# Factorization-machine scorer on Trainium2: the weights, the parameters and the first columns of the input in one transfer instead of three

## The chip, the cores and the metric

The kernel runs on one core of one Trainium2 chip. The metric is the device time of one execution in microseconds (us); lower is better. On that core five engines run their own instruction streams and meet at semaphores: TensorE (PE, with its weight loads as PEld), VectorE (DVE), ScalarE (ACT), GpSimd (POOL) and SyncE (SP), which here issues every DMA transfer. Sixteen DMA engines carry the bytes.

## The reference

The input x is float32, 1024 samples by 12500 features. With a factor matrix F (12500 x 16), linear weights w (12500) and a small three-layer network (16 to 128 to 64 to 1):

```python
x_reg = x @ W_lin.T + b_lin
emb = x @ factors
sum_squared = jnp.square(emb.sum(axis=1))
squared_sum = (jnp.square(x) @ jnp.square(factors)).sum(axis=1)
h = relu(emb @ W1.T + b1)
h = relu(h @ W2.T + b2)
y = x_reg + 0.5 * (sum_squared - squared_sum)[:, None] + h @ W3.T + b3
return (0.5 + sigmoid(y) * 5.0).squeeze()
```

So each feature is multiplied by 17 weights (16 factors and the linear one), and its square by one weight, the row sum of the squared factors. x is 51.2 MB and is read once; everything else is small.

## The kernel before

x lies transposed in HBM, features on the 128 partitions. The 12500 features are 97 chunks of 128 and a remainder of 84. The first chunk (`xf`, 128 x 1024) and the remainder (`xl`, three sets of 32 features, laid out as 128 x 768) are handled ahead of everything. The other 96 chunks come in groups of 8 chunks by 512 samples, 2 MB each: 12 groups for the first half of the samples, then 8 for the second half. They go through a ring `xr` of RING = 4 slots. The last 32 chunks of the second half come as nine smaller end pieces (`x_end`, PIECES) of 352 or 160 samples.

For a group, TensorE multiplies the 8 chunks by their 17 weights into the bank `p_lin` of that half (L467), while VectorE squares three chunks (L394) and ScalarE five (L298) into `sq`; TensorE then multiplies the squares into the same bank. GpSimd copies each group's weights into `wr` (L273) and the row sums of the squared factors into `wz` (L275). After the squares' last matmul TensorE increments `sq_used`, and SP, which waits for it, refills the slot (L242). The half's network layers and the sigmoid follow, for the second half in two blocks of samples, and the result is stored.

SP's queue before the loop holds, in this order: the head `hd` (L232: the weights of all 97 chunks, the parameters of the network, the weights of the remainder; 128 rows of 7616 B), `xf` (L233: 128 rows of 4096 B), `xl` (L234: 128 rows of 3072 B) and the four first groups (L236: 128 rows of 16384 B each). Each has its own semaphore: `hd_landed`, `first_landed`, `rest_landed`, `x_landed[s]`.

What waits for the three first transfers: VectorE waits for `hd_landed`, computes the squared factors `fsq` (L376), those of the remainder, their row sums `s_all` (L381) and `ws`, the bias (L385), waits for `rest_landed` and squares the remainder (`sql`, L388); then come its groups. ScalarE waits for `first_landed` and squares the first chunk (`sqf`, L290). GpSimd waits for `hd_landed` and for the row sums, copies them to `ws` (L266, L267), and then places weights for the ring. TensorE clears its banks, waits for `hd_landed` and `first_landed` and multiplies the first chunk; waits for `rest_landed` and multiplies the remainder; then the squares of both; then the groups.

Of the kernel before, what the change touches and what calls it, by code (L numbers as in the profile page):

```python
# [6 lines left out]
ACT = mybir.ActivationFunctionType  # L7
# [5 lines left out]
B, N, EMB = 1024, 12500, 16  # L13
H1, H2 = 128, 64
P = 128
LIN = EMB + 1
# [22 lines left out]
REST_K = 32  # L39
REST_SETS = -(-REST // REST_K)  # L40
REST_COLS = B // (P // REST_K)
# [32 lines left out]
C_ALL = C_HALF + 4  # L74


HD_P = ALL * LIN
HD_L = HD_P + C_ALL
HD = HD_L + REST_SETS * LIN


def fm_kernel(nc, head, x_first, x_rest, x_groups, x_end, out):
    with ExitStack() as ctx:
        def sb(name, shape, dt=F32):
            return ctx.enter_context(nc.sbuf_tensor(name, shape, dt))
# [4 lines left out]
        def sem(name):  # L90
            return ctx.enter_context(nc.semaphore(name))

        hd = sb("hd", [P, HD])
        xf = sb("xf", [P, B])
        xl = sb("xl", [P, REST_SETS, REST_COLS])
        xr = sb("xr", [P, RING, CHUNKS, HALF])
        sqf = sb("sqf", [P, B])
        sql = sb("sql", [P, REST_SETS, REST_COLS])
# [11 lines left out]
        rest = sb("rest", [P, BLOCKS[2][1]])  # L110
# [7 lines left out]

        w = hd[:, 0:HD_P].rearrange("p (c k) -> p c k", k=LIN)
        pr = hd[:, HD_P:HD_L]  # L120
        wl = hd[:, HD_L:HD].rearrange("p (c k) -> p c k", k=LIN)

        p_lin = [bank("p_lin0"), bank("p_lin1")]
        p_sq = bank("p_sq")
# [2 lines left out]
        p_h2 = bank("p_h2")  # L127

        hd_landed = sem("hd_landed")
        first_landed = sem("first_landed")  # L130
        rest_landed = sem("rest_landed")
        x_landed = [sem(f"x_landed{s}") for s in range(RING)]
        end_landed = [sem(f"end_landed{i}") for i in range(len(PIECES))]
        y_stored = sem("y_stored")
# [8 lines left out]
        first_squared = sem("first_squared")  # L143
# [28 lines left out]
        def cols(k):  # L172

            c, n = BLOCKS[k]
            return slice(c, c + n)
# [21 lines left out]
        def tot_bank(k):  # L197
            return p_tot[k % 2]
# [5 lines left out]
        def width(i):  # L204
            return BLOCKS[PIECES[i][0]][1]

        def piece(a, i, c, n):

            at = ENDS * (BLOCKS[PIECES[i][0]][0] - HALF)
            return a[:, at + c * width(i):at + (c + n) * width(i)]  # L210
# [5 lines left out]
        def chunks(i):  # L216
            return sum(PIECES[i][2]) + sum(PIECES[i][3])

        def last_slot(i):
            k, c = PIECES[i][:2]  # L220
            return (ENDS * (BLOCKS[k][0] - HALF) + (c + chunks(i)) * BLOCKS[k][1] - 1) // (CHUNKS * HALF)
# [8 lines left out]
        @block.sync  # L230
        def _(sp):
            sp.dma_start(hd[:, :], head).then_inc(hd_landed, 16)  # L232
            sp.dma_start(xf[:, :], x_first).then_inc(first_landed, 16)  # L233
            sp.dma_start(xl[:, :, :].rearrange("p c b -> p (c b)"), x_rest).then_inc(rest_landed, 16)  # L234
            for s in range(RING):
                sp.dma_start(xr[:, s].rearrange("p c b -> p (c b)"), x_groups[s, :, 0:CHUNKS * HALF]).then_inc(x_landed[s], 16)  # L236

            with sp.Fori(1, sum(ROUNDS)) as r:
                for s in range(RING):

                    sp.wait_ge(sq_used, RING * r + s + 1)
                    sp.dma_start(xr[:, s].rearrange("p c b -> p (c b)"),  # L242
                                 x_groups[bass.ds(RING * r + s, 1), :, 0:CHUNKS * HALF].rearrange("g p n -> (g p) n")
                                 ).then_inc(x_landed[s], 16)
            at = 0
            for i in range(len(PIECES)):
                c, n = PIECES[i][1], chunks(i)
                rows = x_end[at:at + P * n * width(i)].rearrange("(p m) -> p m", p=P)
                sp.wait_ge(sq_used, TOTAL + last_slot(i) + 1)
                sp.dma_start(piece(xe, i, c, n), rows).then_inc(end_landed[i], 16)  # L250
                at += P * n * width(i)

            for k in range(len(BLOCKS)):
                sp.wait_ge(y_ready[k], 1)
                sp.dma_start(out[cols(k)].rearrange("(q b) -> q b", q=4), y[0:P:32, line(k)]).then_inc(y_stored, 16)
            sp.wait_ge(y_stored, 16 * len(BLOCKS))
# [28 lines left out]
        @block.scalar  # L285
        def _(act):
            act.wait_ge(zero_set, 1)
            nc.scalar.activation(warm[:, :], zero[:, 0:1], ACT.Sigmoid)
            act.wait_ge(first_landed, 16)
            nc.scalar.activation(sqf[:, :], xf[:, :], ACT.Square).then_inc(first_squared, 1)  # L290

            def squares(r, s):
                act.wait_ge(x_landed[s], 16 * (r + 1))

                act.wait_ge(sq_used, RING * r + s + 1)
                c = BY_DVE
                for n in BY_ACT:
                    nc.scalar.activation(sq[:, s, c:c + n, :], xr[:, s, c:c + n, :],  # L298
                                         ACT.Square).then_inc(act_squared, 1)
                    c += n  # L300

            def square_end(i, j=0):
                c = PIECES[i][1] + sum(PIECES[i][2][:j])
                n = PIECES[i][2][j]
                if j == 0:
                    act.wait_ge(end_landed[i], 16)
                nc.scalar.activation(piece(sq_end, i, c, n), piece(xe, i, c, n),  # L307
                                     ACT.Square).then_inc(act_end_squared, 1)

            def copy_lin(k, u):  # L310
                nc.scalar.copy(lin[:, part(k, u)], p_lin[k][:, u * BLOCKS[k][1] // 2:(u + 1) * BLOCKS[k][1] // 2]  # L311
                               ).then_inc(lin_ready[k], 1)

            def layer1(k, n):
                act.wait_ge(p_h1_done[k], 1)
                c = BLOCKS[k][0]
                nc.scalar.activation(h1[:, c:c + n], p_h1[0][:, 0:n], ACT.Relu,
                                     bias=pr[:, C_B1:C_B1 + 1]).then_inc(h1a_ready[k], 1)

            def embedding_square(k):  # L320
                act.wait_ge(p_es_done[k], 1)
                nc.scalar.activation(gsq[:, line(k)], tot_bank(k)[:, line(k)], ACT.Square).then_inc(gsq_ready[k], 1)

            def sigmoid(k):
                act.wait_ge(p_tot_done[k], 1)
                nc.scalar.activation(sg[:, line(k)], tot_bank(k)[:, line(k)], ACT.Sigmoid,
                                     bias=bias[:, :]).then_inc(sg_ready[k], 1)

            with act.Fori(0, ROUNDS[0]) as r:
                for s in range(RING):  # L330
                    squares(r, s)

            act.wait_ge(sq_used, RING + GROUPS)
            copy_lin(0, 0)
            copy_lin(0, 1)
            layer1(0, BLOCKS[0][1] // 2)
            embedding_square(0)
            act.wait_ge(bias_ready, 1)
            sigmoid(0)

            with act.Fori(ROUNDS[0], sum(ROUNDS)) as r:
                for s in range(RING):
                    squares(r, s)

            square_end(0, 0)
            square_end(0, 1)
            square_end(1, 0)
            square_end(1, 1)
            square_end(2)
            square_end(3)  # L350
            square_end(4, 0)
            act.wait_ge(p_lin_done[1], 1)
            copy_lin(1, 0)
            copy_lin(1, 1)
            nc.scalar.copy(rest[:, :], p_lin[1][:, BLOCKS[1][1]:HALF]).then_inc(rest_copied, 1)
            embedding_square(1)
            square_end(4, 1)
            layer1(1, BLOCKS[1][1])
            square_end(5, 0)
            square_end(5, 1)  # L360
            square_end(6, 0)
            square_end(6, 1)
            square_end(7, 0)
            square_end(7, 1)
            square_end(8)
            sigmoid(1)
            embedding_square(2)
            act.wait_ge(squares_done, 1)
            nc.scalar.copy(qs[:, :], p_sq[:, 0:BLOCKS[LAST][1]]).then_inc(qs_ready, 1)
            sigmoid(2)  # L370

        @block.vector
        def _(dve):
# [10 lines left out]
                                    ).then_inc(s_ready, 1)  # L384
            nc.vector.tensor_tensor(bias[:, :], pr[:, C_BLIN:C_BLIN + 1], pr[:, C_B3:C_B3 + 1],  # L385
                                    ALU.add).then_inc(bias_ready, 1)
            dve.wait_ge(rest_landed, 16)
            nc.vector.tensor_tensor(sql[:, :, :], xl[:, :, :], xl[:, :, :], ALU.mult).then_inc(rest_squared, 1)  # L388

            def squares(r, s):  # L390
# [74 lines left out]
        def _(pe):  # L465
# [15 lines left out]
                return ps[32 * (t % 4):32 * (t % 4) + m, c:c + n]  # L481

            pe.wait_ge(hd_landed, 16)
            pe.wait_ge(first_landed, 16)
            for h in range(2):
                add_mm(quad(p_lin[h], 0, LIN, 0, HALF), w[:, 0, :], xf[:, half(h)])

# [5 lines left out]
                        h, at = divmod(REST_COLS * t, HALF)  # L493
                        add_mm(quad(p_lin[h], t, m, at, REST_COLS), weights[rows, c, :], rhs[rows, c, :])

            pe.wait_ge(rest_landed, 16)
            remainder(LIN, wl, xl)
            pe.wait_ge(ws_ready, 1)
            pe.wait_ge(first_squared, 1)
# [220 lines left out]
```

## Time and profile before

| what | value |
|---|---|
| median of three runs | 134.57 us (134.57 to 134.70) |
| profiled execution | 134.6 us, span 132.4 us from first to last instruction |
| instructions | 2859 |
| TensorE busy | 106.6 us (81%), 1123 matmuls |
| ScalarE, VectorE, GpSimd busy | 64.1, 53.1, 12.5 us |
| DMA | 52.34 MB in 4639 packets, mean 395 GB/s over the span |
| DMA issues | head 952 KB, first chunk 512 KB, remainder 384 KB, 20 groups of 2048 KB, nine end pieces |

How to read it: the span is what the profile covers of one execution; the 2.2 us between it and the time lie around it. Busy time is an average over the span; where a chain of waits goes through DMA, an engine's idle time before it costs nothing. A timeline row gives the start, the duration, the engine, the line of the code, what is written from what, the number of instructions merged into the row, and in brackets how long the engine was idle before it and what ended that.

### The profile page before, as it was taken

To read this page: it belongs to the slowest core of one execution; us is meant where nothing else is said; L and a number is where in the kernel's file an instruction comes from. 1 tells how busy PE (TensorE), PEld (TensorE's weight loads), DVE (VectorE), ACT (ScalarE), POOL (GpSimd) and SP (SyncE) were. 2 spreads that over 40 slices of the span, in tenths; PEclk is the share of its full clock that TensorE was granted. 3 is DMA by queue.
4 is the path that set the end of the run, shared out by engine and by line. 5 is a ranking of instruction groups with operands and counts; after the bars stand their busy time and mean duration, and the time that the engine had idled before them with its cause. 6 is when DMAs were issued, how large, how long until landed. Compare 5 with 4: busy or idle time off the path is not lost.

```text
span 132.4 us, 2859 instructions
## 1 busy us (share of the span) xinstructions
PE 106.6 (81%) x1123; PEld 31.6 (24%) x1123; DVE 53.1 (40%) x51; ACT 64.1 (48%) x72; POOL 12.5 (9%) x48
## 2 busy tenths in 40 slices
PE   6089999768877877877978869996967966989992
PEld 4012222111111211211212312211111111335881
DVE  0392450532531541540540292450451351576571
ACT  4031660734733743742744394652662562465851
POOL 4016001110010011011011001151000000000000
PEclk9999999999999999999999999999999999999998
DMA  4999999999999999999999999999999999999800
GB/s 115 397 460 431 430 431 426 430 426 431 421 435 426 435 426 416 440 426 431 431 426 426 426 430 426 421 440 416 435 421 431 435 418 424 411 411 411 321 13 6
DMA packets 4639, 52.34 MB, mean 395 GB/s; under 512 B 532, under 2 KB 664, under 8 KB 1688
## 3 DMA queue, kind: packets, MB, share of 16 engines
q1 hardware_dynamic: 4632, 52.23, 93.6%
q8 instruction: 6, 0.10, 0.3%
q14 instruction: 1, 0.01, 0.0%
HBM read 52.22 MB, written 0.00 MB: 394 GB/s over the span
## 4 chain that ended last, share of the span: by engine, by line
DMA 63%; PE 28%; SPq 3%; ACT 3%; issue 2%; DVE 1%; ACTq 0%
DMA xr<-in_x_groups 52%; PE p_lin L467 22%; DMA xr<-in_x_end 11%; ACT sq L298 2%; PE p_sq L467 2%; PE p_h L557 2%; SPq L236 1%; PE p_tot L467 1%; PE p_h L588 1%; DVE h L419 0%; DVE h L414 0%; PE p_tot L570 0%; SPq L234 0%; SPq L233 0%; SPq L232 0%
## 5 line engine op out<-in xcount | busy, mean ns | idle before, releaser
L298 ACT ACTIVATE sq<-xr 128x1536 f32<-128x1536 f32 (+1 forms) x40 | 48.5, 1262 | 47.2 <-DMA xr<-in_x_groups 47.2
L394 DVE TENSOR_TENSOR sq<-xr 128x1536 f32<-128x1536 f32 x20 | 35.1, 1758 | 56.6 <-DMA xr<-in_x_groups 56.6
L467 PE MATMUL p_lin<-xr,wr 128*17 128x512 f32 x320 | 38.2, 594 | 13.8 <-DMA xr<-in_x_groups 13.8
L467 PE MATMUL p_lin<-sq,wz 128*18 128x512 f32 x320 | 38.2, 594 | 2.3 <-ACT sq L298 1.0
L467 PEld LDWEIGHTS p_lin<-xr,wr 128*17 128x17 f32 x320 | 7.9, 97 | 42.3 <-issue 21.6
L467 PEld LDWEIGHTS p_lin<-sq,wz 128*18 128x18 f32 x320 | 8.2, 97 | 31.5 <-ACT sq L298 16.9
L273 POOL COPY wr<-hd x20 | 7.4, 372 | 71.5 <-PE p_lin L467 70.8
L402 DVE TENSOR_TENSOR sq<-xr 128x320 f32<-128x320 f32 (+5 forms) x15 | 10.4, 724 | 8.1 <-DMA xr<-in_x_end 8.1
L307 ACT ACTIVATE sq<-xr 128x320 f32<-128x320 f32 (+5 forms) x15 | 9.1, 652 | 7.1 <-DMA xr<-in_x_end 7.1
L467 PE MATMUL p_lin<-xr,hd 128*17 128x352 f32 (+1 forms) x128 | 10.0, 380 | 1.5 <-DMA xr<-in_x_end 1.5
L467 PE MATMUL p_lin<-sq,ws 128*18 128x352 f32 x64 | 6.6, 459 | 0.0
L467 PE MATMUL p_lin<-xf,hd 128*17 128x512 f32 x4 | 3.6, 1049 | 3.5 <-DMA xf<-in_x_first 3.5
L467 PEld LDWEIGHTS p_lin<-xr,hd 128*17 128x17 f32 x128 | 4.3, 97 | 5.5 <-issue 3.6
L467 PE MATMUL p_sq<-sq,ws 128*18 128x160 f32 x64 | 4.1, 300 | 0.0
L275 POOL COPY wz<-s_all x20 | 3.9, 196 | 0.0
L376 DVE SCALAR_TENSOR_TENSOR fsq<-hd 128x1552 f32<-128x1552 f32 x1 | 1.8, 1775 | 4.4 <-DMA hd<-in_head 4.4
L290 ACT ACTIVATE sqf<-xf 128x1024 f32<-128x1024 f32 x1 | 1.1, 1057 | 4.7 <-DMA xf<-in_x_first 4.7
L467 PEld LDWEIGHTS p_lin<-sq,ws 128*18 128x18 f32 x64 | 2.4, 97 | 2.3 <-issue 1.4
L557 PE MATMUL p_h<-lin,hd 128*32 128x256 f32 (+2 forms) x32 | 2.4, 384 | 0.5 <-ACT lin L311 0.5
L467 PEld LDWEIGHTS p_sq<-sq,ws 128*18 128x18 f32 x64 | 2.5, 98 | 0.3
L414 DVE TENSOR_SCALAR h<-p_h,hd 128x256 f32<-128x256 f32 (+1 forms) x2 | 0.9, 434 | 4.0 <-PE p_h L557 4.0
L467 PE MATMUL p_lin<-xl,hd 32*17 32x256 f32 x24 | 2.3, 535 | 0.0
(50 smaller groups left out, 34.7 us busy)
## 6 DMA issues: line engine op xcount, KB each, us to landing
xr<-in_x_groups SPq DMA_DIRECT2D x20, 2048.0 KB, 15.4
xr<-in_x_end SPq DMA_DIRECT2D x1, 2112.0 KB, 10.8
xr<-in_x_end SPq DMA_DIRECT2D x3, 640.0 KB, 12.3
xr<-in_x_end SPq DMA_DIRECT2D x1, 1760.0 KB, 14.6
xr<-in_x_end SPq DMA_DIRECT2D x1, 1056.0 KB, 12.7
hd<-in_head SPq DMA_DIRECT2D x1, 952.0 KB, 4.8
xr<-in_x_end SPq DMA_DIRECT2D x1, 704.0 KB, 14.1
xf<-in_x_first SPq DMA_DIRECT2D x1, 512.0 KB, 5.7
```

What stands on the lines that cost most here:

```text
L236: sp.dma_start(xr[:, s].rearrange("p c b -> p (c b)"), x_groups[s, :, 0:CHUNKS * HALF]).then_inc(x_landed[s], 16)
L273: nc.gpsimd.tensor_copy(wr[:, bass.ds(s, 1), :, :].rearrange("p s c k -> p (s c) k"), w[:, bass.ds(at, CHUNKS), :]).then_inc(wr_ready, 1)
L275: nc.gpsimd.tensor_copy(wz[:, bass.ds(s, 1), :, LIN:WZ].rearrange("p s c k -> p (s c k)"), s_all[:, bass.ds(at, CHUNKS)]).then_inc(wz_read ...
L290: nc.scalar.activation(sqf[:, :], xf[:, :], ACT.Square).then_inc(first_squared, 1)
L298: nc.scalar.activation(sq[:, s, c:c + n, :], xr[:, s, c:c + n, :], ACT.Square).then_inc(act_squared, 1)
L307: nc.scalar.activation(piece(sq_end, i, c, n), piece(xe, i, c, n), ACT.Square).then_inc(act_end_squared, 1)
L376: nc.vector.scalar_tensor_tensor(fsq[:, :, :], w[:, :, 0:EMB], -0.5, w[:, :, 0:EMB], ALU.mult, ALU.mult).then_inc(fsq_ready, 1)
L394: nc.vector.tensor_tensor(sq[:, s, 0:BY_DVE, :], xr[:, s, 0:BY_DVE, :], xr[:, s, 0:BY_DVE, :], ALU.mult).then_inc(dve_squared, 1)
L402: nc.vector.tensor_tensor(piece(sq_end, i, c, n), piece(xe, i, c, n), piece(xe, i, c, n), ALU.mult).then_inc(dve_end_squared, 1)
L467: return nc.tensor.matmul(out, lhsT, rhs, start=False, stop=False, skip_group_check=True)
L557: mm = nc.tensor.matmul(bank[32 * t:32 * t + 32, 0:n], pr[:, C_W1 + 32 * t:C_W1 + 32 * t + 32], rhs, start=True, stop=True, skip_group_che ...
L588: mm = nc.tensor.matmul(p_h2[32 * t:32 * t + 32, row(k)], pr[:, C_W2 + t % 2 * 32:C_W2 + t % 2 * 32 + 32], h1[:, part(k, t // 2)], start=T ...
```

## The change

The first chunk and the remainder of x are put behind the weights in each of the head's 128 rows, which become 14784 B long. `xf` and `xl` are slices of the tile `hd`; the two transfers and their semaphores go, and each engine that waited for one of them has `hd_landed` instead, or nothing where it had that wait already. No other instruction changes.

```diff
 HD_P = ALL * LIN
 HD_L = HD_P + C_ALL
-HD = HD_L + REST_SETS * LIN
+HD_F = HD_L + REST_SETS * LIN
+HD_R = HD_F + B
+HD = HD_R + REST_SETS * REST_COLS
...
-        xf = sb("xf", [P, B])
-        xl = sb("xl", [P, REST_SETS, REST_COLS])
...
-        wl = hd[:, HD_L:HD].rearrange("p (c k) -> p c k", k=LIN)
+        wl = hd[:, HD_L:HD_F].rearrange("p (c k) -> p c k", k=LIN)
+        xf = hd[:, HD_F:HD_R]
+        xl = hd[:, HD_R:HD].rearrange("p (c b) -> p c b", b=REST_COLS)
...
             sp.dma_start(hd[:, :], head).then_inc(hd_landed, 16)
-            sp.dma_start(xf[:, :], x_first).then_inc(first_landed, 16)
-            sp.dma_start(xl[:, :, :].rearrange("p c b -> p (c b)"), x_rest).then_inc(rest_landed, 16)
...
-            act.wait_ge(first_landed, 16)
-            nc.scalar.activation(sqf[:, :], xf[:, :], ACT.Square).then_inc(first_squared, 1)
+            act.wait_ge(hd_landed, 16)
+            nc.scalar.activation(sqf[:, :], xf, ACT.Square).then_inc(first_squared, 1)
...
-            dve.wait_ge(rest_landed, 16)
             nc.vector.tensor_tensor(sql[:, :, :], xl[:, :, :], xl[:, :, :], ALU.mult).then_inc(rest_squared, 1)
...
             pe.wait_ge(hd_landed, 16)
-            pe.wait_ge(first_landed, 16)
...
-            pe.wait_ge(rest_landed, 16)
             remainder(LIN, wl, xl)
...
+    head[:, HD_F:HD_R] = xT[:P]
+    head[:, HD_R:] = rest.reshape(REST_SETS, REST_K, P // REST_K, REST_COLS).transpose(2, 1, 0, 3).reshape(P, -1)
```

## Rows read from the trace of the kernel before

**Rows 1.** The page: span, and gigabytes per second in 40 equal slices.
```profile
span 132.4 us, 2859 instructions
...
GB/s 115 397 460 431 430 431 426 430 426 431 421 435 426 435 426 416 440 426 431 431 426 426 426 430 426 421 440 416 435 421 431 435 418 424 411 411 411 321 13 6
```

**Rows 2.** The chain of waits in order of time: start us, us, what.
```profile
101.64 14.59 DMA xr<-in_x_end
...
116.28 6.75 PE p_lin L467 x92
```

**Rows 3.** VectorE's timeline: groups 1 to 4 and 20, then two end pieces.
```profile
12.87 1.76 DVE L394 TENSOR_TENSOR sq<-xr 128x1536 f32<-128x1536 f32 x1 [2.54 <-DMA xr<-in_x_groups]
17.78 1.76 DVE L394 TENSOR_TENSOR sq<-xr 128x1536 f32<-128x1536 f32 x1 [3.15 <-DMA xr<-in_x_groups]
23.86 1.76 DVE L394 TENSOR_TENSOR sq<-xr 128x1536 f32<-128x1536 f32 x1 [4.31 <-DMA xr<-in_x_groups]
28.76 1.76 DVE L394 TENSOR_TENSOR sq<-xr 128x1536 f32<-128x1536 f32 x1 [3.14 <-DMA xr<-in_x_groups]
...
107.08 1.76 DVE L394 TENSOR_TENSOR sq<-xr 128x1536 f32<-128x1536 f32 x1 [3.16 <-DMA xr<-in_x_groups]
...
122.15 0.90 DVE L402 TENSOR_TENSOR sq<-xr 128x320 f32<-128x320 f32 x2 [0.64 <-DMA xr<-in_x_end]
123.73 0.89 DVE L402 TENSOR_TENSOR sq<-xr 128x320 f32<-128x320 f32 x2 [0.69 <-DMA xr<-in_x_end]
```

**Rows 4.** The timeline of SP's issues.
```profile
0.75 0.40 SPq L232 DMA_DIRECT2D hd<-in_head  x1
...
1.66 0.44 SPq L234 DMA_DIRECT2D xl<-in_x_rest  x1
2.15 2.25 SPq L236 DMA_DIRECT2D xr<-in_x_groups  x4
19.83 3.76 SPq L242 DMA_DIRECT2D xr<-in_x_groups  x2
```

**Rows 5.** DMA queues: packets, MB, share of 16 engines over the span.
```profile
q8 instruction: 6, 0.10, 0.3%
```

**Rows 6.** DMA issues: size, median us from issue to landing.
```profile
xl<-in_x_rest SPq DMA_DIRECT2D x1, 384.0 KB, 6.2
```

**Rows 7.** The timeline of all engines from 0 to 26 us.
```profile
5.59 1.77 DVE L376 SCALAR_TENSOR_TENSOR fsq<-hd 128x1552 f32<-128x1552 f32 x1 [4.44 <-DMA hd<-in_head]
6.92 1.06 ACT L290 ACTIVATE sqf<-xf 128x1024 f32<-128x1024 f32 x1 [4.67 <-DMA xf<-in_x_first]
...
7.03 3.57 PE L467 MATMUL p_lin<-xf,hd 128*17 128x512 f32 x4 [3.51 <-DMA xf<-in_x_first]
...
9.38 0.95 DVE L388 TENSOR_TENSOR sql<-xl 128x768 f32<-128x768 f32 x1
9.46 0.91 POOL L266 COPY ws<-s_all 128x1 f32<-128x1 f32 x1 [7.57 <-DVE ws L383]
...
12.76 1.89 PE L467 MATMUL p_lin<-sqf,ws 128*18 128x512 f32 x4
...
15.99 1.91 PE L467 MATMUL p_lin<-xr,wr 128*17 128x512 f32 x16
...
23.86 1.91 PE L467 MATMUL p_lin<-xr,wr 128*17 128x512 f32 x16 [0.81 <-DMA xr<-in_x_groups]
```

**Rows 8.** Stretches: us, busy times, granted clock, DMA share, GB/s.
```profile
1.50:2.00 0.50, 0.50 (x4) 0.35 (x3) 0.00 (x0) 0.50 (x1) 0.40 (x1) 1.00 1.02 137
2.00:2.50 0.50, 0.50 (x5) 0.35 (x3) 0.00 (x0) 0.23 (x2) 0.00 (x0) 1.00 0.32 76
2.50:3.00 0.50, 0.50 (x4) 0.38 (x3) 0.00 (x0) 0.00 (x0) 0.00 (x0) 1.00 0.75 259
3.00:3.50 0.50, 0.50 (x3) 0.04 (x1) 0.00 (x0) 0.00 (x0) 0.00 (x0) 1.00 0.90 381
3.50:4.00 0.50, 0.02 (x1) 0.00 (x0) 0.00 (x0) 0.00 (x0) 0.00 (x0) 1.00 1.10 457
```

More of the change, by code:

```diff
@@ L78, with fm_kernel @@
 HD_L = HD_P + C_ALL
-HD = HD_L + REST_SETS * LIN
-def fm_kernel(nc, head, x_first, x_rest, x_groups, x_end, out):
+HD_F = HD_L + REST_SETS * LIN
+HD_R = HD_F + B
+HD = HD_R + REST_SETS * REST_COLS
+def fm_kernel(nc, head, x_groups, x_end, out):
     with ExitStack() as ctx:
@@ L129, in fm_kernel @@
         hd_landed = sem("hd_landed")
-        first_landed = sem("first_landed")
-        rest_landed = sem("rest_landed")
         x_landed = [sem(f"x_landed{s}") for s in range(RING)]
@@ L679 @@
     xT = np.asarray(r_input_data).T
-    x_first = np.ascontiguousarray(xT[:P])
     rest = np.zeros((REST_SETS * REST_K, B), f32)
     rest[:REST] = xT[P:P + REST]
-    x_rest = np.ascontiguousarray(rest.reshape(REST_SETS, REST_K, P // REST_K, REST_COLS).transpose(2, 1, 0, 3).reshape(P, -1))
     chunks = xT[P + REST:].reshape(ALL - 1, P, B)
@@ L711 @@
     params[:, C_B3] = np.asarray(L0_rec_b3)
-    arrays = {"head": head, "x_first": x_first, "x_rest": x_rest, "x_groups": x_groups, "x_end": x_end}
+    arrays = {"head": head, "x_groups": x_groups, "x_end": x_end}
     nc = bacc.Bacc("TRN2", target_bir_lowering=False, num_devices=1)
```

## The prediction

> **What bounds the kernel now.** I read the page first, for the shape of the span: of the 40 slices of the GB/s row, slices 2 to 37 read 397 to 460 [rows 1], so the 16 DMA engines have work from the second slice to the last 10 us. The question is whether a compute engine ever holds that stream up. The chain of waits answers it: its last DMA piece starts at 101.64 us, when SP issues the second end piece, and ends 14.59 us later, at 116.23 us, when that piece lands; from 116.28 us TensorE has it [rows 2]. A transfer of 1.8 MB that takes 14.59 us from issue to landing was queued behind others: VectorE's squares, which each wait for one group, start 4.89 or 4.90 us apart (28.76 minus 23.86; the 16 intervals from 28.76 to 107.08 us are 78.32 us, 4.895 us each, the copy work of the middle included) [rows 3]. So 2,097,152 B in 4.895 us, 428.4 GB/s, is the pace, and about three transfers stand in the queue at a time. SP's refill for slot 0 goes out at 19.83 us, while the groups that land at 23.86 and 28.76 us are still to come [rows 3, 4]: 8.9 us of cover.
>
> The end is therefore: start of the stream + all its bytes at 428.4 GB/s + a fixed tail of about 16 us behind the piece that lands at 116.23 us. The change keeps every byte: 7616 + 4096 + 3072 = 14784 B per row. Only three things can move the end: the start of the stream, the overhead of packets in it, or a compute engine that becomes so late that SP's refills are.
>
> One irregular row matters below. The third group comes 6.08 us after the second (23.86 minus 17.78), not 4.90, and no later interval gives the 1.18 us back [rows 3]. Compute was waiting, so this is in the stream. The queue rows give a candidate: six instruction fetches, 0.3% of 16 engines' 132.4 us, some 6.4 us in all or 1.06 us each [rows 5]. A group counts as landed when the last engine is through, so a fetch on one engine shows in every landing after it. That it was a fetch is my inference.
>
> **The change part by part.**
>
> *Two issues fewer on SP.* Before, SP issues the head at 0.75 us and the first group at 2.15 us [rows 4]. Without the two issues between, the first group goes out when the second transfer did, 0.75 + 0.40 + 0.05 = 1.20 us (0.05 is the gap between 1.66 + 0.44 and 2.15), 0.95 us earlier. That buys nothing while the queue is full: the three first transfers are 1,892,352 B, 4.42 us of streaming, so the first group's descriptors wait either way. If the stream did hang on the issue, it would be worth up to 0.95 us; I take 0.
>
> *256 data packets and 32 completion packets fewer.* From below 0. From the rows: head, first chunk and remainder land at 5.59 us (VectorE's first instruction on it), 6.92 us (ScalarE's square of the first chunk) and 1.66 + 6.2 = 7.86 us (issue and time to landing) [rows 4, 6, 7]. The first chunk took 1.33 us for 524,288 B, which at 428.4 GB/s would be 1.22; the remainder 0.94 us for 393,216 B, at that pace 0.92. Excess 0.11 + 0.02 = 0.13 us. The second estimate: two neighbouring end pieces of 640 KB (655,360 B, 5120 B rows) start VectorE at 122.15 and 123.73 us [rows 3], 1.58 us against 1.53 us at the pace, 0.05 us per transfer, 0.10 for two. I take 0.13 us off, bounds 0 and 0.2.
>
> The Trainium skill, *DMA: Bandwidth & Descriptors*, section on the anatomy of one DMA, fits a software-issued DMA with 2.0 us fixed plus its bytes; the same page advises to merge small transfers. Paid in series, that would take 4 us off and give 130.6 us. The trace disagrees for queued transfers: the second landed 1.33 us after the first, of which its bytes fill 1.22.
>
> *The start of the stream.* In the four half microseconds from 1.5 to 3.5 us it moves at 137, 76, 259 and 381 GB/s [rows 8]: 426 KB, where the pace would give 857 KB, so 431 KB or 1.0 us is lost in the ramp. The order of issue, rows and partitions of this first transfer stay; only its rows are 14784 B instead of 7616 B. If a stall is per row, fewer rows meet it and up to half, 0.5 us, comes back; if it is a latency in time, nothing does. Of the other sign, a longer row could hold a slow engine longer, by the 0.27 us that 7168 B more take on one engine at a sixteenth of the pace. I take 0: the ramp lasts as long as several rows, which looks like a time and not a count of rows (one of 7616 B takes an engine 0.28 us at a sixteenth of the pace, the ramp 1.5 us).
>
> *The head lands later.* All three waits become the one for 7.86 - 0.13 = 7.73 us. What stands behind it:
> - VectorE: from 5.59 us to the end of the remainder's square, 9.38 + 0.95 = 10.33 us, is 4.74 us [rows 7]. From 7.73 us it ends at 12.47 us. The first group lands at 12.87 - 0.13 = 12.74 us [rows 3]. Hidden with 0.27 us to spare; without that cover each us would delay the squares of the first group, not the stream.
> - GpSimd: its first copy of the row sums starts at 9.46 us, after the reductions [rows 7]; later by 7.73 - 5.59 = 2.14 us is 11.60 us, done at 12.51 us. TensorE wants it for the squares of the first chunk, at about 12.76 + 0.83 = 13.59 us [rows 7]. GpSimd's copies for the first slot follow and are wanted at about 16.8 us.
> - ScalarE: 1.06 us from 7.73 us, done at 8.79 us; nothing is due before 12.74 us.
> - TensorE: starts at 7.03 us now and at about 7.86 us then, 0.83 us later; its first group starts at 15.99 us now and at 16.8 us then. The first two groups go back to back, and then TensorE stands idle 0.81 us before the third group's matmuls at 23.86 us [rows 7], which wait for that landing, as do the squares. So 0.83 us late becomes at most 0.02 us there. The refills of slots 0 and 1 go out up to 0.83 us late, against 8.9 us of cover.
> Everything waiting sums to 0 at the end. From the third group on, the changed kernel should be the old one, shifted by the stream.
>
> *The sum.* The profiled execution has a span of 132.4 us and a time of 134.6 us, 2.2 us around it; the runs' median is 134.57. Span 132.4 - 0.13 - 0 - 0 = 132.3; time 134.57 - 0.13 = **134.44 us**, 0.1% less. Differences under 0.2%, 0.27 us, are about what cannot be told from no change here: the three runs already spread over 0.13 us.
>
> **The rivals.**
> - *The ramp shortens.* Half to a quarter of the 1.0 us lost in it comes back, because larger rows keep the slow engines fed: 134.44 - 0.25 to -0.5 = 133.94 to 134.19 us. For it: the ramp is a real loss at the head of the only bound. Against it: its cause isn't in the rows, and the slowest engine, not the mean, makes a landing. Chance 0.19.
> - *The stream hangs on SP's issues.* 0.95 us earlier, 134.57 - 0.95 = 133.62 us. Against it: the rate is already at 457 GB/s between 3.5 and 4.0 us [rows 8], when the last of SP's first groups is only being issued. The skill's fixed cost per transfer, above, would go further the same way. Chance 0.03.
> - *The slip at the third group is dealt otherwise* (slower). The engines leave the ramp staggered, and the slip of 1.18 us counts from the engine that was hit. The packets of the first transfer change that stagger, the dropped instructions change when code is fetched. If the fetch falls on the engine that is already last, or two fall on one, landings from there on are later by up to another 1.18 us: 134.44 + 1.18 = 135.62 us. It decides from 0.40 us more slip on (0.27 + the 0.13 gained). For it: a single engine sets all later landings. Against: three runs within 0.13 us, so the deal is steady for one program. Chance 0.10. By the same mechanism the other way, a hit on an engine that leads, down to 134.44 - 1.18 = 133.26 us: chance 0.04. The Trainium skill, *DMA: Bandwidth & Descriptors*, section on queues, rings and completion order, has each engine take turns between its queues by packets and a transfer complete only with its last engine; no row here shows an engine by itself.
> - *The late head reaches the stream* (slower). TensorE's 0.83 us would pass whole to the end only if every group left it no idle time: 134.44 + 0.83 = 135.27 us. Against it, the idle 0.81 us before the third group, and more later. Chance 0.04.
>
> **How the numbers follow.** The forecast case, 134.3 to 134.8 us, has 0.60; the cases below it 0.19 + 0.03 + 0.04 = 0.26; the cases above 0.10 + 0.04 = 0.14. Faster by over 0.2% (below 134.30) 0.26, within 0.60, slower (above 134.84) 0.14. The range: 133.9 leaves out the issue rival and most of the lucky slip, 134.95 the upper two thirds of the unlucky one and most of the late head, together under 0.2. The forecast case's own range is 134.3 to 134.6 us.
>
> **What would show it.** SP issues the first group near 1.2 us; the head lands at 7.7 us, not before 7.4; VectorE's prologue ends before its first group, which starts at 12.7 us; the first multiply of a group at 16.8 us; the third group's matmuls within 0.2 us of its landing; intervals of 4.90 us from there on; the last end pieces 0.1 us earlier. The forecast is wrong if the ramp's sum to 3.5 us differs from 426 KB by over 100 KB, or if the landing of the third group isn't 23.7 us with all later ones moved alike.

## The result: slower by 0.3%

Over 20 runs each, the changed kernel took 135.35 us (median) and the kernel before 134.78; the ratio is 1.003, 95% interval 1.0018 to 1.0042. So it is slower, by 0.24 to 0.57 us, where 134.44 us and "within 0.2%" were forecast, and 135.35 us lies outside the range given, 133.9 to 134.95 us. The 20 times of the changed kernel lie in two clusters: 8 from 134.59 to 135.04 us, 12 from 135.31 to 135.78. Those of before fill 134.57 to 135.00 without a gap. The profiled execution is one of the upper cluster, 135.31 us with a span of 133.3 us, so the profiles differ by 0.7 us in time and 0.9 in span, more than the medians.

The page of the changed kernel: the same bytes, 288 packets fewer.

```profile
span 133.3 us, 2856 instructions
...
DMA packets 4351, 52.34 MB, mean 393 GB/s; under 512 B 500, under 2 KB 632, under 8 KB 1272
...
q8 instruction: 6, 0.10, 0.3%
```

The timeline of all engines up to 26 us, beside [rows 7]:

```profile
0.75 0.39 SPq L233 DMA_DIRECT2D hd<-in_head  x1
...
1.21 2.56 SPq L235 DMA_DIRECT2D xr<-in_x_groups  x4
...
8.53 1.06 ACT L289 ACTIVATE sqf<-hd 128x1024 f32<-128x1024 f32 x1 [6.28 <-DMA hd<-in_head]
...
8.55 4.76 PE L465 MATMUL p_lin<-hd 128*17 128x512 f32 x28 [5.03 <-DMA hd<-in_head]
...
12.31 0.95 DVE L386 TENSOR_TENSOR sql<-hd 128x768 f32<-128x768 f32 x1
12.40 0.91 POOL L265 COPY ws<-s_all 128x1 f32<-128x1 f32 x1 [10.50 <-DVE ws L382]
...
13.65 1.72 POOL L274 COPY wz<-s_all  x1
...
16.61 1.91 PE L465 MATMUL p_lin<-xr,wr 128*17 128x512 f32 x16
...
20.45 7.30 SPq L241 DMA_DIRECT2D xr<-in_x_groups  x3
...
23.48 1.90 PE L465 MATMUL p_lin<-xr,wr 128*17 128x512 f32 x16
```

VectorE has the head at 8.53 us, not at 7.73. What follows it is hidden as foreseen: VectorE is through at 12.31 + 0.95 = 13.26 us, before its first group, TensorE starts that group at 16.61 us and the third one at 23.48 us, 0.18 us behind its landing, and SP's first refill goes out 0.62 us late against eight microseconds of cover.

VectorE's timeline, groups 1 to 4, 16 to 18 and 20 (L392), beside [rows 3]. Each square waits for the landing of its group, so its start tells the landing:

```profile
13.52 1.79 DVE L392 TENSOR_TENSOR sq<-xr 128x1536 f32<-128x1536 f32 x1 [0.25 <-DMA xr<-in_x_groups]
18.43 1.76 DVE L392 TENSOR_TENSOR sq<-xr 128x1536 f32<-128x1536 f32 x1 [3.12 <-DMA xr<-in_x_groups]
23.30 1.76 DVE L392 TENSOR_TENSOR sq<-xr 128x1536 f32<-128x1536 f32 x1 [3.12 <-DMA xr<-in_x_groups]
28.64 1.76 DVE L392 TENSOR_TENSOR sq<-xr 128x1536 f32<-128x1536 f32 x1 [3.58 <-DMA xr<-in_x_groups]
...
87.54 1.90 DVE L392 TENSOR_TENSOR sq<-xr 128x1536 f32<-128x1536 f32 x1 [3.15 <-DMA xr<-in_x_groups]
93.44 1.76 DVE L392 TENSOR_TENSOR sq<-xr 128x1536 f32<-128x1536 f32 x1 [4.00 <-DMA xr<-in_x_groups]
98.17 1.76 DVE L392 TENSOR_TENSOR sq<-xr 128x1536 f32<-128x1536 f32 x1 [2.98 <-DMA xr<-in_x_groups]
...
107.97 1.76 DVE L392 TENSOR_TENSOR sq<-xr 128x1536 f32<-128x1536 f32 x1 [3.14 <-DMA xr<-in_x_groups]
```

And in the kernel before, groups 16 to 18:

```profile
87.49 1.76 DVE L394 TENSOR_TENSOR sq<-xr 128x1536 f32<-128x1536 f32 x1 [3.13 <-DMA xr<-in_x_groups]
92.39 1.76 DVE L394 TENSOR_TENSOR sq<-xr 128x1536 f32<-128x1536 f32 x1 [3.14 <-DMA xr<-in_x_groups]
97.28 1.76 DVE L394 TENSOR_TENSOR sq<-xr 128x1536 f32<-128x1536 f32 x1 [3.14 <-DMA xr<-in_x_groups]
```

The second group is 18.43 - 17.78 = 0.65 us late. The pace behind it is the old one, 4.9 us a group, with the irregular intervals (the slips) elsewhere: before, one of 6.08 us ahead of the third group; here 5.34 us ahead of the fourth, 5.90 us ahead of the seventeenth and 4.73 us behind that. So the 0.65 us is not simply carried along. At the fourth group the changed kernel is 0.12 us ahead (28.64 against 28.76 us), at the sixteenth 0.05 us behind (87.54 against 87.49); the loss appears at the seventeenth, 93.44 against 92.39 us, and 0.89 us of it is left at the twentieth (107.97 against 107.08). From there on both kernels are alike: the chain of waits shows the second end piece and then TensorE to the end, 16.1 us as in [rows 2].

```profile
102.53 14.61 DMA xr<-in_x_end
117.18 6.75 PE p_lin L465 x92
```

The stream's rate in the ramp, beside [rows 8] (the last two figures are the DMA share and GB/s):

```profile
1.50:2.00 0.50, 0.50 (x4) 0.34 (x3) 0.00 (x0) 0.50 (x1) 0.40 (x1) 1.00 1.92 355
2.00:2.50 0.50, 0.50 (x5) 0.35 (x3) 0.00 (x0) 0.23 (x2) 0.00 (x0) 1.00 0.46 89
2.50:3.00 0.50, 0.50 (x4) 0.38 (x3) 0.00 (x0) 0.00 (x0) 0.00 (x0) 1.00 0.74 177
3.00:3.50 0.50, 0.50 (x3) 0.03 (x1) 0.00 (x0) 0.00 (x0) 0.00 (x0) 1.00 0.69 296
3.50:4.00 0.50, 0.01 (x1) 0.00 (x0) 0.00 (x0) 0.00 (x0) 0.00 (x0) 1.00 0.79 325
```

To 3.5 us these are 458 KB, before 426; to 4.0 us 621 KB, before 655. The bytes in sum are nearly the same. A packet counts in the stretch in which it starts (so a DMA share of 1.92 is possible), which flatters long rows; and the last engine, which makes the landing, is not to be seen in a mean.

It is to be seen in the trace's completion times. The trace keeps 16 of them for each transfer, without saying which DMA engine each belongs to. Those of the second group lie at 17.06 to 17.65 us before the change, median 17.37. In the changed kernel 14 of them lie at 16.95 to 17.48 us, median 17.28, and two at 18.18 and 18.30 us. The packet line from 17.75 to 18.40 us, of the kernel before and then of the changed one, shows those two as its packets under 512 B:

```profile
DMA packets 16, 0.26 MB, mean 403 GB/s; under 512 B 0, under 2 KB 0, under 8 KB 0
```

```profile
DMA packets 20, 0.29 MB, mean 454 GB/s; under 512 B 2, under 2 KB 2, under 8 KB 2
```

So two of the 16 engines leave the ramp late; the others are not late at all. The packet times of the trace show where: a row of 14784 B takes 0.55 us in the full stream, but one that starts at 1.90 us takes 2.31 us. Before the change a row takes 0.29 us in the full stream and the longest one of the ramp 1.22 us.

### The profile page after: what moved, and what is told of

It reads as the page before. It is cut to its first block, busy times and chain, and to the rows that moved or that the text cites. A ratio compares the mean times of both kernels' runs of the same rounds, so it can differ in the third digit from the quotient of the medians.

```text
span 133.3 us, 2856 instructions
## 1 busy us (share of the span) xinstructions
PE 105.3 (79%) x1123; PEld 31.4 (24%) x1123; DVE 53.3 (40%) x51; ACT 64.1 (48%) x72; POOL 15.1 (11%) x48
## 4 chain that ended last, share of the span: by engine, by line
DMA 64%; PE 27%; ACT 3%; SPq 2%; issue 2%; DVE 1%; ACTq 0%
DMA xr<-in_x_groups 53%; PE p_lin L465 22%; DMA xr<-in_x_end 11%; ACT sq L297 2%; PE p_h L553 2%; PE p_sq L465 2%; SPq L235 1%; PE p_tot L465 1%; PE p_h L584 1%; DVE h L417 0%; DVE h L412 0%; PE p_tot L566 0%; SPq L233 0%; ACT lin L310 0%; ACT sg L325 0%
## 5 line engine op out<-in xcount | busy, mean ns | idle before, releaser
L392 DVE TENSOR_TENSOR sq<-xr 128x1536 f32<-128x1536 f32 x20 | 35.2, 1766 | 54.4 <-DMA xr<-in_x_groups 54.3
L465 PE MATMUL p_lin<-hd 32*17 32x256 f32 (+1 forms) x28 | 4.8, 464 | 5.0 <-DMA hd<-in_head 5.0
L274 POOL COPY wz<-s_all x20 | 7.0, 350 | 0.0
L289 ACT ACTIVATE sqf<-hd 128x1024 f32<-128x1024 f32 x1 | 1.1, 1057 | 6.3 <-DMA hd<-in_head 6.3
L465 PEld LDWEIGHTS p_lin<-hd 32*17 32x17 f32 (+1 forms) x28 | 1.0, 97 | 8.8 <-DMA hd<-in_head 5.5
```

Of the source, the lines that this page charges most:

```text
L274: nc.gpsimd.tensor_copy(wz[:, bass.ds(s, 1), :, LIN:WZ].rearrange("p s c k -> p (s c k)"), s_all[:, bass.ds(at, CHUNKS)]).then_inc(wz_read ...
L289: nc.scalar.activation(sqf[:, :], xf, ACT.Square).then_inc(first_squared, 1)
L392: nc.vector.tensor_tensor(sq[:, s, 0:BY_DVE, :], xr[:, s, 0:BY_DVE, :], xr[:, s, 0:BY_DVE, :], ALU.mult).then_inc(dve_squared, 1)
L465: return nc.tensor.matmul(out, lhsT, rhs, start=False, stop=False, skip_group_check=True)
```

## The experiments

Theory A, with which I went into the experiments: the long rows leave the DMA engines further apart behind the ramp, and an instruction fetch on an engine that is already late costs time. Rival B: the late start of compute moves the fetches. Rival C: the groups, issued 0.95 us earlier, disturb the first transfer.

All times in us. "Second", "sixteenth" and "twentieth" are the starts of VectorE's square of that group in the profile, "longest" the longest interval between two groups after 80 us, "profiled" the profiled execution's time. Each ratio is to the kernel before as it ran beside that version; its median there was 134.58 to 134.78 us, so the ratios can be compared and the medians less so.

| run | rows of the first transfer | second | sixteenth | longest | twentieth | profiled | median | ratio to before (95%) |
|---|---|---|---|---|---|---|---|---|
| before | 7616 B | 17.78 | 87.49 | 4.91 | 107.08 | 134.6 | 134.78 | |
| changed | 14784 B | 18.43 | 87.54 | 5.90 | 107.97 | 135.31 | 135.35 | 1.003 (1.0018 to 1.0042) |
| e1 | 7616 B | 17.84 | 87.66 | 4.91 | 107.24 | 134.62 | 134.71 | 1.0003 (0.9993 to 1.0013) |
| e2 | 7616 B | 17.97 | 87.13 | 5.76 | 107.60 | 135.05 | 134.43 | 0.9986 (0.9976 to 0.9997) |
| e3 | 14784 B | 18.20 | 87.45 | 5.86 | 107.85 | 135.15 | 135.16 | 1.0038 (1.0023 to 1.0052) |
| e4 | 1024, then 13760 B | 18.33 | 87.39 | 6.05 | 107.96 | 135.22 | 135.26 | 1.0039 (1.0025 to 1.0054) |
| e5, e11, e12, e16 (changed) | 14784 B | 18.36, 18.13, 18.25, 18.53 | 87.34, 87.37, 87.51, 87.24 | 5.77, 5.85, 5.86, 6.18 | 107.80, 107.76, 107.90, 108.13 | 135.15, 135.17, 135.28, 135.50 | | |
| e6 | 7616 B | 17.91 | 87.27 | 5.05 | 107.02 | 134.67 | 134.68 | 0.9997 (0.9988 to 1.0007) |
| e7 | 7616 B | 17.81 | 87.38 | 5.38 | 107.45 | 134.79 | 134.68 | 0.999 (0.9978 to 1.0003) |
| e8 | 16384 B | 18.31 | 87.44 | 5.07 | 107.23 | 134.58 | 134.78 | 1.0016 (1.0005 to 1.0026) |
| e9 | 3696 B | 17.62 | 87.36 | 5.04 | 107.11 | 134.53 | 134.62 | 1.0005 (0.9996 to 1.0014) |
| e10 | 14784 B | 18.23 | 87.41 | 5.67 | 107.77 | 135.06 | 135.19 | 1.0038 (1.0026 to 1.0051) |
| e13 | 7616 B | 17.77 | 87.61 | 4.91 | 107.21 | 134.68 | 134.73 | 1.001 (0.9996 to 1.0024) |
| e14 | 14784 B | 18.39 | 87.66 | 4.90 | 107.24 | 135.92 | 134.95 | 1.0038 (1.0003 to 1.0073) |
| e15 (as e2) | 7616 B | 17.71 | 87.31 | 5.26 | 107.28 | 134.64 | 134.77 | 1.0013 (0.9999 to 1.0027) |

**e1, the waits alone.** The three transfers of before on one semaphore; all engines wait for all of them.

```diff
-            sp.dma_start(xf[:, :], x_first).then_inc(first_landed, 16)
+            sp.dma_start(xf[:, :], x_first).then_inc(hd_landed, 16)
...
-            dve.wait_ge(hd_landed, 16)
+            dve.wait_ge(hd_landed, 48)
```

> The three transfers of the kernel before, with the waits of the changed one: every engine waits for all three before it starts. Theory A (the long rows of the first transfer leave the DMA engines further apart in the ramp, and an instruction fetch on an engine that is already late is what costs): the row lengths are those of before, so the last of the three lands at 7.85 us, the first group at 12.87 us, no interval of 5.9 us near 93 us, and the time is that of before, 134.6 to 134.9 us. Rival B (the late start of compute is the cause, by moving when code is fetched): first group at 12.87 us, but an interval of 5.9 us near 93 us in most runs, 135.3 us. Rival C (the groups issued 0.95 us earlier disturb the first transfer): as A.

Measured: all three landed by 7.93 us, first group 12.93 us, no time lost. The late start of compute costs nothing; rival B falls.

**e2, the same tile in two column parts.**

```diff
-            sp.dma_start(hd[:, :], head).then_inc(hd_landed, 16)
+            for c in (slice(0, HD_F), slice(HD_F, HD)):
+                sp.dma_start(hd[:, c], head[:, c]).then_inc(hd_landed, 16)
```

> The changed kernel with its 14784 B rows loaded by two transfers of 7616 B and 7168 B of each row, both counted on the one semaphore that all engines wait for. Theory A: both land by 7.85 us (8.53 us in the changed kernel), first group near 12.8 us, time 134.6 to 134.9 us. Rival B: lands early too, but 135.3 us by the fetches. Rival C: between, as the groups are issued 0.5 us earlier than before instead of 0.95: landing near 8.2 us.

Measured: landed by 8.07 us, second group 17.97, 134.43 us. The merged tensor and its pitch stay, and the loss in the median is gone. One of its executions, the profiled one, still had a long interval of 5.76 us and took 135.05 us.

**e3, the groups issued as late as before.** `sp.wait_ge(pads_set, 2)` ahead of the groups; they go out at 1.92 us.

> The changed kernel, but SP waits for GpSimd's two clears (about 1.95 us) before it issues the first group, so that the groups go out near 2.0 us, as before the change (2.15), instead of 1.21. Rival C: the transfer is undisturbed in its ramp, lands near 7.8 us, first group 12.8 us, time 134.7 us. Theory A: nothing changes, landing at 8.5 us, first group 13.5 us, most runs 135.3 us. B as A for the time.

Measured: head at 8.31 us, 135.16 us. The earlier issue isn't the cause; rival C falls.

**e4, short rows ahead.** Column parts of 1024 B and 13760 B.

> The changed kernel with a short transfer ahead: the first 1024 B of each row, then the other 13760 B, both counted on the one semaphore. Theory A, if only the rows in flight in the first 1.3 us matter: the short rows carry the ramp and the stagger shrinks below that of before; landing at or before 7.9 us, first group 12.8 us or earlier, time 134.5 to 134.8 us. If the long rows behind them are caught by the ramp as well (1024 B take an engine 0.04 us each): landing near 8.5 us and 135.3 us as in the changed kernel. B: 135.3 us in any case.

Measured: as the changed kernel, with the head at 8.44 us. VectorE's timeline:

```profile
8.44 1.78 DVE L376 SCALAR_TENSOR_TENSOR fsq<-hd 128x1552 f32<-128x1552 f32 x1 [7.30 <-DMA hd<-in_head]
```

Long rows right behind a short transfer are caught too.

**e5, e11, e12, e16, the changed kernel again**, for profiles of both clusters.

> The changed kernel itself, for one more profile. Its 20 times lay in two clusters, 8 between 134.59 and 135.04 and 12 between 135.31 and 135.78. Theory A1 (the ramp's stagger alone costs the time): the head lands at 7.9 us in a run near 134.7, and at 8.5 us in one near 135.4. Theory A2 (the stagger is always there, and the time is lost when an instruction fetch near 90 us falls on an engine that is late): the head lands near 8.5 us whatever the time, and the interval of 5.9 us near 93 us is there only in a run near 135.4 us.

> The changed kernel for one more profile, hoped to be of its lower cluster (134.6 to 135.0 us, 8 of 20 times). Theory A2: second group at work near 18.4 us whatever the time, and in the lower cluster no landing interval over 5.3 us after 80 us. Theory A1: in the lower cluster the second group is at work before 18.0 us.

> As the third profile of the changed kernel: A2, second group near 18.4 us in either cluster, a landing interval of 5.7 to 6.1 us after 80 us only in the upper one; A1, second group before 18.0 us in the lower one.

> The changed kernel for one more profile, hoped to be of its lower cluster. If the ramp's lag is always there: second group at work near 18.3 us and, where the time is under 135.05 us, no landing interval over 5.3 us after 80 us. If the ramp is what differs: second group before 18.0 us.

A1 says that the late ramp alone costs the time, A2 that it is always there and costs only when a fetch meets a late engine. All four took 135.15 us or more. In each the second group is late and one interval near 93 or 98 us is 5.77 to 6.18 us. No profile of the lower cluster was had, so A1 and A2 aren't told apart by these.

**e6, more code on SP.** 288 satisfied waits ahead of SP's loop.

> The kernel before, with 288 waits on the head's semaphore in SP's program between the first groups and the loop: SP has nothing to do there until 19.8 us, and the waits are satisfied, so they add only code, 288 instructions. If instruction fetches occupy an engine of the stream: 7 or 8 fetches instead of 6, and at least one landing interval of the groups grows from 4.90 to between 5.2 and 6.2 us beside the one before (6.08); time from 134.64 us by 0 if the hit engine leads and isn't hit again, up to 136.2 us if it is the last. If fetches don't disturb the stream: intervals and time as before, with 7 or 8 fetches.

Measured: the profile counts 144 instructions more (3003 against 2859), still six fetches in the instruction queue q8, and no loss. The added code brought no further fetch, so the test misses its object.

**e7, two transfers, two semaphores**, so that VectorE starts at 5.73 us.

> Two transfers with short rows, as in the run with column halves (134.43 us), but with a semaphore each, so that VectorE and GpSimd start on the weights at 5.6 us as before the change. If the 0.2 us that the column halves gained on the kernel before come from fewer packets in the stream: 134.4 us again, first group near 12.9 us. If they come from the late start of compute: 134.64 us.

**e15, e2 once more.**

> The changed kernel with its rows loaded in column parts of 7616 and 7168 B, once more (134.43 us against 134.64 the first time). If that gain was real: ratio 0.9975 to 0.9997 again. If it was chance: 0.999 to 1.001.

Measured: e7 0.999 with an interval that reaches 1, e15 1.0013. The gain of e2 didn't repeat; no version here is shown to beat the kernel before.

**e8, a group ahead of everything.**

> The kernel before, but SP issues the first group (rows of 16384 B) ahead of head, first chunk and remainder. Theory A (long rows in the ramp spread the engines, whoever they belong to): the first group, 2 MB, lands not at 1.77 + 0.9 + 4.9 = 7.6 us but 0.6 us or more later, at 8.2 to 9.0 us, and the stream keeps that lag: 135.2 us or more if the late start of compute costs nothing. Rival (it is something of the merged tensor itself, its pitch of 14784 B or its size): the first group lands near 8.0 us and the time is 134.6 to 134.8 us.

Measured: second group 18.31 us although the tensors are those of before, so long rows at the start of the stream are late whoever they belong to. The last completion of the group issued first is at 8.73 us, in the range expected by A. But the time rose only by 0.16%, where A expected 135.2 us or more: the twentieth group is at 107.23 us. A late ramp doesn't have to reach the end.

**e9, four column parts of 3696 B.**

> The changed kernel with its rows loaded in four column parts of 3696 B, all on the one semaphore. Dose and response for the length of the rows in the ramp: the second group was at work at 17.78 us with rows of 7616 B, 17.97 with two parts of about 7.4 KB, 18.43 with 14784 B. If the length of the rows sets how far the engines leave the ramp apart: 17.4 to 17.7 us here, and 134.2 to 134.5 us. If only rows above some length are caught, 17.8 us and 134.4 to 134.7 us.

Measured: second group 17.62 us, 0.16 us earlier than before the change; 134.62 us, no gain at the end.

**e10, 64 satisfied waits more in TensorE's program.**

```diff
+            for _ in range(64):
+                pe.wait_ge(zero_set, 1)
             pe.wait_ge(hd_landed, 16)
```

> The changed kernel with 64 satisfied waits more in TensorE's program, where it idles for the head (3.5 to 8.5 us): only the place of all later code moves, by 64 instructions. If the fetches are TensorE's and their deal decides the time: the fetches stand at other times than 22.7, 77.3 and 91.1 us or are more or fewer, the long landing intervals go with them, and the time's cluster changes: 134.7 us if the hits fall on engines in front, 135.4 to 136 us if two fall on a late one. If the fetches have no part in the lost time: second group at 18.4 us, 135.35 us as before.

The queue rows of short windows show where a fetch starts. The changed kernel from 77 to 79 us and from 90 to 92 us:

```profile
q8 instruction: 1, 0.02, 3.2%
...
q8 instruction: 1, 0.02, 3.4%
```

In e10 the windows 73 to 75 and 87 to 89 us have those two fetches, and the windows above have none. In the five profiles of the changed kernel they start at 77.12 to 77.41 and at 90.95 to 93.16 us, here at 73.62 and 87.90 us. Code added to TensorE alone (32 instructions more in the profile, 2888 against 2856) moved them by 3 us or more: they are fetches of TensorE's code. The time stayed that of the changed kernel (135.19 us).

**e13 and e14, before and changed with short group loops.** Both keep two of eight chunks' matmuls in the group loops, for x and for its squares, so the sums leave out 72 of the 96 chunks' terms.

```diff
-                for c in range(CHUNKS):
+                for c in range(2):
```

> The kernel before with most of the groups' matmuls left out: two of eight chunks for x and two of eight for its squares, so the output leaves out 72 of 96 chunks' terms in the group loops. The bytes, the squares and SP's refills stay, TensorE's loops are a quarter as long. If the fetches in the stream are those of TensorE's code: fewer of the six before 110 us, and the slip of 6.08 us or others missing or moved; second group at 17.8 us. Time 133.0 to 134.6 us: with no fetch on a late engine up to 1.1 us less than 134.6.

> The changed kernel with the same matmuls left out as in the run before this one (72 of 96 chunks' terms missing). Second group at 18.3 to 18.4 us. If the ramp's lag alone costs the time: 0.5 to 0.7 us above the kernel before with short loops, in one cluster. If it only costs with a fetch on a late engine and no fetch falls in the stream: also 0.6 us above, as the last engine's lag from the ramp then is the lag at the end. If fetches fall on engines in front only: within 0.2 us of it. With a fetch on a late engine: 1.0 us above and more.

There are four fetches now, and one of them before 110 us: in e13 in the window 33 to 35 us, in e14 in 66 to 69 us. VectorE's timeline of e13, groups 2, 3, 5 and 6:

```profile
17.77 1.76 DVE L394 TENSOR_TENSOR sq<-xr 128x1536 f32<-128x1536 f32 x1 [3.14 <-DMA xr<-in_x_groups]
22.64 1.76 DVE L394 TENSOR_TENSOR sq<-xr 128x1536 f32<-128x1536 f32 x1 [3.12 <-DMA xr<-in_x_groups]
...
32.44 1.77 DVE L394 TENSOR_TENSOR sq<-xr 128x1536 f32<-128x1536 f32 x1 [3.15 <-DMA xr<-in_x_groups]
38.63 1.76 DVE L394 TENSOR_TENSOR sq<-xr 128x1536 f32<-128x1536 f32 x1 [4.42 <-DMA xr<-in_x_groups]
```

and of e14, groups 2, 12, 14 and 20:

```profile
18.39 1.76 DVE L392 TENSOR_TENSOR sq<-xr 128x1536 f32<-128x1536 f32 x1 [3.12 <-DMA xr<-in_x_groups]
...
67.33 1.79 DVE L392 TENSOR_TENSOR sq<-xr 128x1536 f32<-128x1536 f32 x1 [3.14 <-DMA xr<-in_x_groups]
...
77.86 1.76 DVE L392 TENSOR_TENSOR sq<-xr 128x1536 f32<-128x1536 f32 x1 [0.57 <-DMA xr<-in_x_groups]
...
107.24 1.76 DVE L392 TENSOR_TENSOR sq<-xr 128x1536 f32<-128x1536 f32 x1 [3.14 <-DMA xr<-in_x_groups]
```

The slip of [rows 3] ahead of the third group is gone from e13 (4.87 us there) and stands where its one fetch stands, 6.19 us ahead of the sixth group. In e14 the two intervals from group 12 to 14 take 10.53 us instead of 9.79. So the slips go with the fetches. And the ramp's 0.62 us between the two kernels at the second group is 0.03 us at the twentieth (107.21 and 107.24): the slip was 1.3 us in one and 0.74 us in the other. The times of the pair say less. e13 took 134.73 us, none of the gain of up to 1.1 us that was thought possible. e14's profiled execution took 135.92 us, 1.24 us more than e13's, and little of that is the stream's: VectorE starts on the second end piece 0.05 us later than in e13 and on the third 0.28 us later. Of the chain of waits TensorE has the end, in e13 from 116.40 us on and in e14 already from 112.31 us:

```profile
116.40 6.75 PE p_lin L467 x92
```

```profile
112.31 12.07 PE p_lin L465 x144
```

Stretches of e13 and then of e14 from 110 to 115 us:

```profile
110.00:115.00 5.00, 3.43 (x43) 1.28 (x44) 2.42 (x2) 2.06 (x2) 0.00 (x0) 1.00 0.99 418
```

```profile
110.00:115.00 5.00, 4.29 (x24) 0.97 (x24) 2.43 (x2) 2.06 (x2) 0.00 (x0) 0.50 0.98 415
```

TensorE, with most of its matmuls gone from the loops, had a granted clock of 0.50 there, the lower of its two levels (1.2 GHz), in e14 and 1.00 in e13.

**What each fetch did, from the completion times.** The 16 completion times of a group, moved on by two intervals of 4.895 us, are those of the group two later to about 0.01 us. Where a fetch lies between, one of them is late by 1.49 to 1.57 us and the other 15 stay. That holds for the 50 fetches ahead of the twentieth group in the 18 profiles, but for one: at the first fetch of e8 a second time is 0.67 us late as well. So I take each completion time as that of one DMA engine, and a fetch delays one engine. How far the landing moves follows: by the 1.55 us less the time by which the hit engine was ahead of the last one, or not at all. (In some profiles the hit engine is 1.70 us late at first and gives 0.15 us back in the next group, which is the interval of 4.73 us.) The third fetch of the stream, near 92 us (in e10 at 87.90 us), in the 16 profiles that have one:

| profiles | hit engine, us behind the first of the 16 | us ahead of the last | landing moved by, us |
|---|---|---|---|
| before, e1 | 0.07, 0.19 | 1.71, 1.78 | 0, 0 |
| e6 | 0.31 | 1.39 | 0.16 |
| e9 | 0.35 | 1.38 | 0.17 |
| e8 | 0.06 | 1.35 | 0.20 |
| e15, e7, e2 | 0.73, 0.81, 0.92 | 1.15, 1.03, 0.68 | 0.39, 0.50, 0.88 |
| changed, e5, e11, e12, e16 | 1.26, 1.15, 1.15, 1.16, 1.39 | 0.70, 0.67, 0.75, 0.75, 0.25 | 0.84, 0.88, 0.81, 0.81, 1.29 |
| e3, e4, e10 | 1.22, 1.10, 1.15 | 0.73, 0.55, 0.78 | 0.81, 0.99, 0.79 |

Followed from group to group, the hit engine of the last three rows is in each of the 11 profiles one of the two that were last at the second group. There these two are 1.13 to 1.56 us behind the first engine with the long rows of the last two rows, and 0.75 to 0.98 us in e15, e7 and e2. Why the fetch falls on one of them isn't known.

## Why the prediction was wrong

*What bounds the kernel.* Right. In every profile but e14's the time is the twentieth group's start plus 27.2 to 27.7 us; the end is the stream's.

*Two issues fewer, 0.* Right (e3).

*The packets, -0.13 us.* Not shown. It is below what the repeats tell apart: e2 and e15, one kernel with 144 packets fewer, gave 0.9986 and 1.0013. The median of the second group's 16 completion times is 17.17 to 17.37 us in the four profiles with three first transfers and 17.16 to 17.29 us in the eight with one.

*The start of the stream, "I take 0".* This step failed. I reasoned with the mean rate of the ramp and took it as one figure for all engines, where a landing needs the last engine. The bound of the other sign was 0.27 us; the second group was 0.65 us late, and over the ten profiles with rows of 13.8 KB or more at the start the second group stands at 18.13 to 18.53 us, over the eight with 7.6 KB or less at 17.62 to 17.97. Row length alone does it: e2 against the changed kernel, e8 against before. The waits (e1) and the time of issue (e3) don't. An engine whose long row falls into the slow first microseconds is held by it: the longest row there took 1.62 to 2.47 us in the ten profiles (0.51 to 0.61 us in the full stream) and 0.85 to 1.62 us in the eight. A short transfer ahead doesn't help (e4). Why the ramp is slow isn't known.

*The late head, 0.* The end of it was right: all of it was hidden, although the head came 0.80 us later than foreseen.

*The slip at the third group, left as it was.* This failed with it. "From the third group on, the changed kernel should be the old one" holds up to the sixteenth group, within 0.12 us (28.64 against 28.76, 87.54 against 87.49), not behind it. The rival on the slower side, with 0.10, had the mechanism: a fetch on an engine that is already late. The argument against it, that the deal is steady for one program, says nothing of a changed program. In the kernel before, the first fetch put its engine 1.2 us behind the rest, and the third one, at 93.17 us, hit an engine 1.71 us ahead of that and cost nothing. In the changed kernel the first fetch brought its engine to the same place, so the 0.65 us of the ramp was covered; the third one, at 91.16 us, hit one of the two late engines and moved the landing by 0.84 us. In all five profiles of the changed kernel it did so, at 90.95 to 93.16 us, for 0.81 to 1.29 us. The Trainium skill, *DMA: Bandwidth & Descriptors*, section on queues, rings and completion order, lets an engine take turns between its queues. The same page of the Trainium skill, section on why a DMA increments its semaphore by 16 and not by 1, has the engines finish independently and a transfer complete only with the last of them. The completion times here agree: 15 keep step and one falls behind.

The same account covers e8 and e14, whose ramp was late and whose twentieth group was not: no fetch met one of the two engines that were last at the second group. It would also give the two clusters, if the lower one, 134.59 to 135.04 us, is the executions in which the third fetch misses the late engines. That step is open: none of the five profiles was of the lower cluster.

So the long rows cost nothing by themselves up to the sixteenth group. They leave two engines late, and a fetch on one of these costs the stream that bounds everything 0.8 to 1.3 us in each of the five profiles. Between the medians it is 0.57 us.

## What to carry to other kernels

When a DMA stream sets the end, fewer and longer transfers at its start aren't free: a landing is made by the last of the 16 engines, and an engine that leaves the ramp late stays late, in the changed kernel's profile from the second group to the twentieth. It costs nothing as long as another engine is later still; a fetch of instructions on top of it does cost. Merging saved nothing here that could be measured and lost about half a microsecond; loading the same tile in two column parts took the loss in the median back. Look at the intervals between landings, not at mean rates, and compare two kernels at several groups along the stream: a lag at the second group and a lag at the twentieth need not be the same one.

## What the runs showed of the hardware

- Rows of 14 to 16 KB as the first ones of a stream made the second 2 MB group 0.5 us later than rows of 3.7 to 7.6 KB, for the same bytes in the stream up to it (means of ten and eight profiles, 18.32 and 17.80 us). In the changed kernel's profile that was two completion times of 16; the median one was not later.
- One 16 KB fetch of TensorE's code has a packet time of 0.98 to 1.11 us in the full stream and delays one DMA engine by 1.49 to 1.57 us (50 fetches in 18 profiles). A landing moves by what is left of that once the engine's lead over the last one is used up: 0 (before, at 93.17 us) to 1.3 us (e13, at 34.08 us). The lag was still there at the twentieth group.
- A GpSimd copy that takes 0.20 us by itself took 1.72 us in the changed kernel, from 13.65 us on, while VectorE's square ran from 13.52 to 15.31 us.
